# Quadrant tiles for the score pass, v and logits in one pass, and copies moved from ScalarE to VectorE

## The reference

```python
xn = layernorm(x)
q, k, v = split(xn @ w_in.T + b_in)
attn = softmax(q * scale @ k.T + causal)          # per head
a = where(isnan(o), 0, o), o = (attn @ v) @ w_out.T + b_out
scores = softmax(xn @ gate_w.T); combine = the 2 largest, renormalised, * 2.5
g = silu(xn @ w_gate[e]) * (xn @ w_up[e]);  y = sum_e combine[e] * (g @ w_down[e])
out = x + a + y + shared_swiglu(xn)
```

## Time and profile before

| | |
|---|---|
| median of 3 runs | 625.84 us |
| profiled execution | 626.86 us, span 625.1 us |
| TensorE (PE) busy | 553.6 us, 89% |
| VectorE (DVE) | 466.0 us, 75% |
| GpSimd (POOL) | 352.3 us, 56% |
| ScalarE (ACT) | 346.0 us, 55% |
| weight loads (PEld) | 311.6 us, 50% |
| granted TensorE clock, mean | 0.97 of full |

### The profile page before, as it was taken

One profiled execution on the slowest core, in us unless ns is written; L12 is line 12 of the kernel. 1 busy time (PEld: TensorE's weight loads), 2 busy tenths in 40 slices (PEclk: granted clock), 3 DMA queues, 4 the chain that ended last, 5 costly groups with the idle time before them and its releaser, 6 DMA issues.

```text
span 625.1 us, 12489 instructions
## 1 busy us (share of the span) xinstructions
PE 553.6 (89%) x4144; PEld 311.6 (50%) x4144; DVE 466.0 (75%) x781; ACT 346.0 (55%) x472; POOL 352.3 (56%) x357
## 2 busy tenths in 40 slices
PE   1336999999999999999999999999999999999884
PEld 1223664466525664466535664466534664366421
DVE  3974887589785997589775997589776997489602
ACT  1511349733794349733794349733794349733591
POOL 3332764468454764468454774568454774468442
PEclk9757999999999999999999999999999999999897
DMA  5928103540037003450037102450047002450000
GB/s 142 315 60 192 37 1 105 151 138 18 29 126 196 40 17 105 140 146 17 19 134 195 42 17 104 133 154 17 9 144 202 35 17 104 137 152 18 4 2 17
DMA packets 42854, 56.71 MB, mean 91 GB/s; under 512 B 4400, under 2 KB 28304, under 8 KB 42704
## 3 DMA queue, kind: packets, MB, share of 16 engines
q1 hardware_dynamic: 42832, 56.43, 31.0%
HBM read 41.21 MB, written 14.81 MB: 90 GB/s over the span
## 4 chain that ended last, share of the span: by engine, by line
PE 66%; DVE 12%; issue 7%; ACT 5%; SPq 4%; DMA 4%; POOL 1%; POOLq 0%; DVEq 0%; ACTq 0%
PE banks L579 10%; PE banks L450 7%; PE banks L452 6%; PE banks L451 6%; PE banks L552 6%; PE banks L479 6%; PE banks L461 5%; ACT probs L769 5%; PE banks L470 4%; DVE neg_max L1077 4%; PE banks L463 3%; PE banks L462 3%; DMA cb<-c_dram 2%; DVE max_parts L1097 2%; DVE probs L1059 1%
## 5 line engine op out<-in xcount | busy, mean ns | idle before, releaser
L1077 DVE TENSOR_REDUCE neg_max<-banks 128x2 f32<-128x1024 f32 (+3 forms) x224 | 194.6, 914 | 33.7 <-PE banks L470 32.9
L832 POOL TENSOR_TENSOR probs<-probs,cb 128x512 f32<-128x512 f32 x88 | 115.7, 1315 | 77.0 <-ACT probs L721 72.9
L769 ACT ACTIVATE probs<-banks 128x1024 f32<-128x1024 f32 x160 | 154.2, 1032 | 8.6 <-PE banks L552 7.0
L865 POOL TENSOR_SCALAR_AFFINE_SELECT probs<-probs 128x512 f32<-128x512 f32 x128 | 93.3, 749 | 100.0 <-ACT probs L769 99.7
L838 POOL TENSOR_TENSOR hid_lo<-probs,hid_hi 128x512 fp32r<-128x512 f32 (+1 forms) x88 | 112.9, 1284 | 64.9 <-ACT hid_hi L728 64.9
L721 ACT ACTIVATE probs<-banks 128x512 f32<-128x512 f32 (+1 forms) x112 | 66.9, 598 | 143.5 <-PE banks L452 142.2
L1059 DVE TENSOR_TENSOR probs<-probs,banks 128x512 f32<-128x512 f32 (+1 forms) x112 | 75.5, 680 | 34.3 <-PE banks L452 15.1
L450 PE MATMUL banks<-x_hi,w_hi 128*128 128x512 f32 (+1 forms) x224 | 94.1, 420 | 4.5 <-DVE w_lo L1212 2.7
L728 ACT ACTIVATE hid_hi<-probs 128x512 fp32r<-128x512 f32 (+1 forms) x112 | 70.3, 628 | 47.7 <-DVE probs L1059 46.6
L579 PE MATMUL banks<-probs,v_op 128*32 128x512 f32 (+3 forms) x1024 | 95.2, 444 | 0.3
L452 PE MATMUL banks<-x_hi,w_lo 128*128 128x512 f32 (+1 forms) x224 | 89.5, 399 | 0.0
(11 more groups left out here) (114 smaller groups left out, 602.0 us busy)
## 6 DMA issues: line engine op xcount, KB each, us to landing
cb<-c_dram SPq DMA_DIRECT2D x32, 256.0 KB, 4.5
q_op<-q_dram SPq DMA_DIRECT2D x32, 192.0 KB
k_op<-k_dram SPq DMA_DIRECT2D x32, 192.0 KB
cb<-c_dram SPq DMA_DIRECT2D x16, 224.0 KB, 4.6
q_dram<-q_parts SPq DMA_DIRECT2D x8, 384.0 KB, 2.5
k_dram<-k_parts SPq DMA_DIRECT2D x8, 384.0 KB, 2.5
cb<-c_dram SPq DMA_DIRECT2D x16, 192.0 KB, 4.3
cb<-c_dram SPq DMA_DIRECT2D x16, 160.0 KB, 4.6
```

The costliest lines, as they stand in the source:

```text
L769: nc.scalar.activation(probs[:, g % 2, 2 * u:2 * u + 2, :], ring[:, at:at + 2, :], ACT.Exp).then_inc(exp_done, 1)
L832: nc.gpsimd.tensor_tensor(sg[k % 3][:, :], sg[k % 3][:, :], cb[:, TILE_ORDER[k], :], ALU.mult).then_inc(weighted, 1)
L865: return nc.gpsimd.affine_select(out=view, in_=view, compare_op=ALU.is_ge, fill=0.0, base=0, pattern=[[0, 4], [1, P]], channel_multiplier=-1)
L1077: return nc.vector.tensor_reduce(out, in_, AX.X, ALU.max, negate=True)
```

## The change

Five things change together.

1. The tiles of the score pairs are 64 x 64: each head and each mask product is cut in two by the query half c, so that the four combinations of a and c lie on the four quadrants of the array. The mask is one 64 x 64 identity times one triangle of 64 rows; for c = 1 it covers 64 columns in place of 128. A semaphore increment stands in front of each pair.
2. v and the logits come from one set of 4 matmuls of 136 columns, in round 14, into the two banks 4 and 5; q then uses bank 5 (bank 7 in the first block). The routing weights are transposed by one transpose of 128 x 32, and copied as 32 x 128.
3. The pairs come sooner: pairs 0 and 1 stand at the end of `attend`, each ahead of a `gate_up`, and the others in rounds 1 to 10. The first block has two in each of rounds 2 to 11. `ONE_SLOT` is 7. `transpose_on` and `project_out` stand ahead of the late pair of rounds 2 and 3. `find_numbers` and `finish_output` go to round 14.
4. y and q are copied out of their banks by VectorE, behind v and k.
5. SyncE sends the maxima ahead of the store and then waits for the store to land, which `add_tokens` of the next block waits for (`base_free`). Unit 0's exponential, no longer unit 0's matmul, waits for the last hidden tile.

```diff
-PAIRS_AT = [int(k in (1, 11)) + 2 * int(2 <= k <= 10) for k in range(NT + 2)]
-ONE_SLOT = 5
+PAIRS_FIRST = [2 * int(2 <= k <= 11) for k in range(NT + 2)]
+PAIRS_AT = [int(k in (0, 10)) + 2 * int(1 <= k <= 9) for k in range(NT + 2)]
+ONE_SLOT = 7
...
+        vl = banks[:, 4:6, 0:2 * (E + NE)].rearrange("p a (b c) -> p a b c", b=2)
+        q_bank = banks[:, 5, :]
...
-                before(sp, stored, 16 * b)
...
+                maxima_in(i + 1)
                 store(i)
-                maxima_in(i + 1)
+                sp.wait_ge(stored, 16 * i + 16)
+                apart(sp, base_free)
...
+            def project_q(j, bank):
+                if bank is q_bank:
+                    pe.wait_ge(v_done, j + 1)
+                    pe.wait_ge(router_step, ROUTER_STEPS * j + 2)
+                pe.matmul(bank, wqk_sb[:, 0, :], xnT[:, :], start=True, stop=True).then_inc(q_ready, 1)
...
+            def project_v_and_logits(j):
                 pe.wait_ge(xnT_done, j + 1)
                 before(pe, mrows_done, j)
                 for q in range(QT):
-                    mm = pe.matmul(bank_m[:, q * NE:(q + 1) * NE], xnT[:, q * P:(q + 1) * P], gate_sb[:, :],
+                    mm = pe.matmul(vl[:, q // 2, q % 2, :], xnT[:, q * P:(q + 1) * P], wvg_sb[:, :],
                                    start=True, stop=True)
...
-                for q in range(QT):
-                    mm = pe.transpose(bank_m[0:NE, q * P:(q + 1) * P], comb[:, q, :], ident_sb[:, :])
+                pe.transpose(bank_m[0:QT * NE, 0:P], comb[:, :, :].rearrange("p q e -> p (q e)"), ident_sb[:, :]
...
+            def mask_scores(bank, a, c, at, stride, nblk):
                 own = slice(HALF * a, HALF * (a + 1))
+                cols = slice(at % stride + HALF * c, at % stride + P)
+                blocks = bank[HALF * c:HALF * (c + 1), a, :].rearrange("p (k n) -> p k n", n=stride)
+                return pe.matmul(blocks[:, at // stride:at // stride + nblk, cols], ident_half[own, :],
+                                 mask_half[own, 0:P - HALF * c].unsqueeze(1).to_broadcast([HALF, nblk, P - HALF * c]),
+                                 start=False, stop=True, tile_position=(HALF * a, HALF * c), skip_group_check=True)
+            def head_scores(bank, a, c, h, qt, at, first):
                 own = slice(HALF * a, HALF * a + SROWS)
                 n = (qt + 1) * P
+                rows = slice(HALF * c, HALF * (c + 1))
+                pe.matmul(bank[rows, a, at:at + n], q_op[own, h // 2, qt * P + HALF * c:qt * P + HALF * (c + 1)],
+                          k_op[own, h // 2, 0:n], start=first, stop=False,
+                          tile_position=(HALF * a, HALF * c), skip_group_check=True)
...
+                apart(pe, pe_passed)
...
+                    for c in range(2):
+                        for a in range(2):
+                            head_scores(bank, a, c, 4 * g + j + a, qt, at, m == 0)
+                for c in range(2):
                     for a in range(2):
-                for last in range(2):
-                    for a in range(2):
-                        mm = mask_scores(bank, a, *masks, last)
+                        mm = mask_scores(bank, a, c, *masks)
...
-                n = 0
+                pairs_at = PAIRS_FIRST if i is None else PAIRS_AT
+                n = 0 if i is None else EARLY
...
-                    late = int(k < 4 and PAIRS_AT[k] > 1)
-                    for _ in range(PAIRS_AT[k] - late):
+                    ahead = int(k < EARLY and i is not None)
+                    late = int(2 <= k < 4)
+                    for _ in range(pairs_at[k] - ahead - late):
...
                             project_k(b + 1)
-                            logits(b + 1)
+                            project_v_and_logits(b + 1)
...
                     if k >= 2:
                         down(b, k - 2, i)
+                    if k == 2 and i is not None:
+                        transpose_on(i)
+                    if k == 3 and i is not None:
+                        project_out(i)
...
                         if front and g == GROUPS and u in (2, 3):
+                            pair(i + 1, i, u - 2)
                             gate_up(i + 1, u - 2)
...
# ScalarE, attend
+                        if n == 0:
+                            act.wait_ge(hid_done, NT * i + NT)
...
-                        if (g, u) == (0, 1):
-                            take_y(i)
...
-                            if (g, u) == (0, 3):
-                                take_q(i + 1)
...
# VectorE
+            def take_y(i):
+                dve.wait_ge(down_done, NT * i + NT)
+                nc.vector.tensor_copy(yT[:, :], bank_y[:, :]).then_inc(y_taken, 1)
+            def take_q(j):
+                dve.wait_ge(q_ready, j + 1)
+                nc.vector.tensor_scalar(qk_f[:, 0, :], q_bank, QSCALE, bq_scaled[:, 0:1], ALU.mult, ALU.add
+                                        ).then_inc(q_done, 1)
...
-                dve.wait_ge(m_loaded, 32 * b + 32)
+                dve.wait_ge(base_free, b + 1)
...
+                    if k == NT and i is not None:
+                        find_numbers(i)
+                        finish_output(i)
...
-                    for _ in range(PAIRS_AT[k]):
+                    for m in range(pairs_at[k]):
+                        if k == 1 and m == 1 and i is not None:
+                            take_o(i, 1)
                         pair(b, n)
...
                 if front:
+                    take_v(i + 1)
                     split_k(i + 1)
-                    take_v(i + 1)
+                take_y(i)
+                if front:
+                    take_q(i + 1)
                     split_q(i + 1)
```

More of the change, by code:

```diff
@@ L161, in block_kernel @@
         after = 2 * FT + NT * E
-        mask_f = early[:, after:after + 2 * P].rearrange("p (a n) -> p a n", a=2)
-        ident_f = early[:, after + 2 * P:after + 4 * P].rearrange("p (a n) -> p a n", a=2)
+        mask_f = early[:, after:after + P]
+        ident_f = early[:, after + P:after + P + HALF]
         att = probs[:, 0, 0, :].rearrange("p (q e) -> p q e", q=QT)
@@ L257, in block_kernel @@
         summed = sem("summed")
+        base_free = sem("base_free")
         stored = sem("stored")
@@ L406, in project_k @@
                 pe.matmul(nat[:, 1, :], wqk_sb[:, 1, :], xnT[:, :], start=True, stop=True).then_inc(k_ready, 1)
-            def project_q(j):
-                pe.wait_ge(xnT_done, j + 1)
-                pe.matmul(nat[:, 0, :], wqk_sb[:, 0, :], xnT[:, :], start=True, stop=True).then_inc(q_ready, 1)
-            def project_v(j):
-                pe.wait_ge(router_step, ROUTER_STEPS * j + 2)
-                for q in range(QT):
-                    mm = pe.matmul(bank_m[:, q * P:(q + 1) * P], xnT[:, q * P:(q + 1) * P], wv_sb[:, :],
-                                   start=True, stop=True)
-                mm.then_inc(v_ready, 1)
-            def logits(j):
+            def project_q(j, bank):
[4 more added lines that the diff above has]
+            def project_v_and_logits(j):
                 pe.wait_ge(xnT_done, j + 1)
@@ L429, in transpose_comb @@
                 pe.wait_ge(v_done, j + 1)
-                for q in range(QT):
-                    mm = pe.transpose(bank_m[0:NE, q * P:(q + 1) * P], comb[:, q, :], ident_sb[:, :])
-                mm.then_inc(combT_ready, 1)
+                pe.transpose(bank_m[0:QT * NE, 0:P], comb[:, :, :].rearrange("p q e -> p (q e)"), ident_sb[:, :]
+                             ).then_inc(combT_ready, 1)
             def gate_up(b, k):
@@ L637, in experts_and_maxima @@
                         transpose_maxima(b)
-                    if k == 2 and i is not None:
-                        transpose_on(i)
-                    if k == 3 and i is not None:
-                        project_out(i)
             def attend(i, front):
@@ L648, in attend @@
                         if front and (g, u) == (0, 2):
-                            project_q(i + 1)
-                        if front and (g, u) == (0, 3):
-                            project_v(i + 1)
+                            project_q(i + 1, q_bank)
                         if (g, u) == (0, 3):
@@ L665, in _ @@
             transpose_x(0)
-            logits(0)
-            project_q(0)
+            project_v_and_logits(0)
+            project_q(0, bank_y)
             project_k(0)
-            project_v(0)
             transpose_comb(0)
@@ L784, in _ @@
             act.wait_ge(const_made, 1)
-            take_q(0)
+            take_q(0, bank_y)
             take_k(0)
@@ L1157, in experts_and_maxima @@
                         normalise(b + 1)
-                    if k == 1 and i is not None:
-                        take_o(i, 1)
                     if k == 2 and i is not None:
                         normalise_o(i, 1)
-                    for _ in range(PAIRS_AT[k]):
+                    for m in range(pairs_at[k]):
+                        if k == 1 and m == 1 and i is not None:
```

(8 more changed lines are left out.)

70 lines of the change are left out of this document (30 added, 40 removed).

## The result

The changed kernel takes **637.44 us** (median of 4 runs, 633.21 to 640.25), the kernel before 626.54 beside it (625.79 to 628.87): ratio 1.0163, interval 1.0131 to 1.0195. It is slower by 1.6%. The forecast was 617.0 with a range of 604 to 629, so it missed in sign and the time lies outside the range. The profiled execution took 640.25 (span 638.5), the longest of the four, 13.4 over the profiled one of before. Where some of those 13.4 belong to this one execution, I say so.

A forecast was written before the change was run, and what follows sets the result against it. ScalarE was taken to pace stretch A, TensorE to stream through B and wait for VectorE in C. Block 0 -2.4, six periods -4.2, the seventh -1.6 and the tail -0.6 gave -8.8: 617.0 us, range 604 to 629.

The forecast's parts named there:

- A: Stretch from a block's unit 0 (first transposed scores) to gate_up(0): 22.51 us before, forecast 21.85, 0.65 shorter.
- The wait for the store: SyncE waits for the output's store before writing the next k; a store up to 4.5 us is covered, put at nothing.
- ScalarE's 1.27 us: In A, ScalarE loses the copies of y (0.59) and q (0.68); sixteen exponentials end at 20.8 instead of 21.8.
- Stretch B: From gate_up(0) to gate_up(10), with pairs 1 to 18: 33.75 us before, forecast 33.0.
- Pair 4 and pair 7: Remaining waits in B: pair 4 about 0.4 for pair 3, pair 7 about 0.35 for add_attention.
- The four quadrants: Score pairs: one mask matmul per quadrant, all four at once, saves 1.7 us a block; net -1.1 with added costs.
- The 0.3 set aside for pair 10's operands: In B, pair 10 needs the second half of the operands one round sooner: +0.3.
- The rival of late operands: Chance 0.20: pair 0 waits 0.6 and pair 10 1.0 more for loads; +1.6 a period, 628 us.
- Stretch C: From gate_up(10) to the next unit 0: 14.27 before, forecast 14.97, as the split delays hidden(10) and gate_up(12) waits 1.75.
- The rival in which the split is over in 0.9: Chance 0.25: in C the casts fall between GpSimd's instructions, the split takes 0.9 instead of 2.5; 606.5 us.
- The ends: Block 0 -2.4, the seventh period -1.6, after the last unit 0 -0.6 us.
- the seventh period: Last period, without a next block's front; unit 0's 1.34 wait for the maxima's DMA shrinks as they are ready sooner: -1.6.

The follow-up runs named there:

- before: The kernel before the change, measured beside the changed one: 626.54 us.
- f1: The kernel before, with only find_numbers and finish_output moved to round 14 and the maxima's loads ahead of the store on SyncE: 633.12 us, ratio 1.0099.
- after: The changed kernel, with all five parts of the change: 637.44 us, ratio 1.0163.
- e1: The changed kernel with find_numbers back in round 6 and finish_output back in round 8: 636.55 us, ratio 1.0178.
- e2: The changed kernel with split_maxima moved to round 11, behind hidden(10): 624.20 us, ratio 0.9969.
- e4: The changed kernel with y and q copied by ScalarE again, behind the exponentials of units 1 and 3: 633.67 us, ratio 1.0130.
- h1: g1 with take_v(0) behind split_k(0) ahead of the first block: 617.03 us.
- g2: g1 with y and q copied by ScalarE, behind the exponentials of units 1 and 3: 618.67 us.
- e3: The changed kernel with the edits of both e1 and e2: 619.25 us, ratio 0.9903.
- e5: e3 with y and q copied by ScalarE again: 617.93 us, ratio 0.9869.
- q1: The kernel before with only the 64x64 score tiles and the semaphore increment they need: 622.43 us, ratio 0.9931.
- g1: e2 with find_numbers and finish_output one round earlier, in round 13 ahead of hidden(12): 616.94 us, ratio 0.9854.

## Why the prediction was wrong

**The step that failed**, in its words: "find_numbers and finish_output, moved to round 14, fill 1.4 us in which VectorE now waits for GpSimd; they cost nothing, and at most 0.2 if that wait shrinks." Two things were wrong in it. The wait (1.51 in the row of before, not 1.4) ended 1.22 after find_numbers started (313.34 less 312.12), and the steps need 2.8 from start to hidden(13): 1.77, 0.36 of idle time for find_numbers' result, 0.75 less the overlap. And they ran beside the very multiply for which VectorE waits, where a VectorE pass over two operands took 1.77 instead of 0.68. I had priced this collision for the casts of the split and not for the steps that I called free. The Trainium skill ("GPSIMD Engine Reference", Key points) has a rule for it: GpSimd shares its SBUF interfaces with VectorE, and the two contend where a VectorE instruction reads two SBUF inputs or runs in a two-port mode. The traces agree: find_numbers reads att twice and took 1.77, while the reductions of the maxima and the products of hidden, with their operand in a bank, keep their 1.23 and 0.68 beside GpSimd (the reduction at 373.30 ran beside GpSimd's multiply of 372.82). Read against the step, this rule would have warned me.

Alone the step costs 0.63 a period (f1), in the new order 1.03 (after against e1). Whether it also costs at the end is less sure. With the step in round 14 (after, e2, e4, f1) it is 36.3 to 38.4 from the last unit 0 to the end, without it (the nine others) 34.2 to 37.0, and a half clock near that unit 0 stands in all four of the first but also in before, h1 (6.8 us) and g2. So the 4.2 between e2 and e3 belong in part to the execution.

This step is not the whole miss. Seven times 1.03 is 7.2 us; taken off at no price elsewhere it would leave about 630, still slower than before. The rest of A and the ends, below, hold the larger part of the 22.3, and e1 shows that the old places have a price too.

**The rest of A.** Without that step A is 22.76 (e1, e3), 0.91 above the forecast, in three parts. y came at 4.9 after unit 0 and not at 4.5 (in e3), since split_k's last step took 1.00 instead of 0.69, so that transpose_y waits 0.72 and exponential 4 starts at 5.97 instead of 5.5. An exponential takes 0.964 where I took 0.955, and ScalarE stands once more for 0.24. The exponentials end 21.6 after unit 0, hardly sooner than the 21.8 of before, and pair 0 then adds its 0.4. The wait for the store, which I put at nothing, did cost nothing: k's write is issued at 320.28, as split_k ends (319.25 and 1.00). My assumption that ScalarE's 1.27 us come straight off A was wrong: e4 and e5 show that the copies on VectorE lose a little.

**Stretch B** was 0.45 better than forecast. Pair 4 and pair 7 wait 0.42 and 0.46 (forecast 0.4 and 0.35). q1 puts the tiles at 0.9 in B. The four quadrants run at once as taken. The estimate by the Trainium skill ("TensorEngine Tiling (Array Packing)", Instruction Overhead), 13 us for the 512 extra matmuls, does not show: q1 has all of them and is 0.7% faster. The 0.3 set aside for pair 10's operands wasn't needed in the steady blocks. The rival of late operands is not dead, though: in the second period of the profiled execution pair 10 waited for them, and B had 33.79. In e3's fourth period pair 0, too, waited 0.19 for k_op. Pair 10 in the changed kernel:

```profile
215.00 0.41 PE L480 MATMUL banks<-k_op,q_op 48*64 48x512 bf16 x4 [1.04 <-DMA k_op<-k_dram]
```

**Stretch C** was right in mechanism, place and nearly in size: +0.89 for +0.70, and e2 takes all of it away and 0.9 more. I had forecast this loss and still called the whole a gain. The rival in which the split is over in 0.9 was wrong; it takes 2.6 here, and 3.1 in e2.

**The ends.** Forecast -2.4, -1.6 and -0.6; measured +3.5, +0.3 and +2.7 in this execution. Up to the first unit 0 the nine other traces with the new block 0 have 95.7 to 98.6, those with the old one 95.9, 96.3 (q1) and 96.4: about two of the 3.5 us are this execution's own. In the five traces where unit 0 comes after 97.9, a third stretch of half clock lies behind pair 5's wait of 1.43 (here from 68.4 to 71.8). The other five have the same wait of 1.43 and no such stretch, so the wait alone does not decide it. I forecast "about 1" for that wait and not what the clock can do behind it.

k_op came later because its loads were issued 2.0 later (44.57 instead of 42.53), behind the copy of comb (40.02 instead of 38.01); why they then landed 3.3 later is not shown. Of the 2.0, 1.7 are there already when split_k starts (25.43 instead of 23.76): 0.5 at the statistics that wait for x (15.54, 15.01), the rest behind the 0.66 that VectorE now waits for v and the logits and the 0.6 of take_v, which both stand ahead of split_q. The last two steps of split_k ran beside GpSimd (8.2 us for what takes 1.1), but before it was two steps of the router, 2.88 and 3.84 us, and both pairs are ahead of the copy of comb, so this moved k's write, and the copy of comb by 0.4 at most. h1 moves take_v(0) and leaves GpSimd at the same step.

For the seventh period I took the maxima's load to come sooner; in C it came later, with down(11).

**Sum.** Against the forecast, six periods miss by 1.94 in A, -0.45 in B and 0.19 in C (10.1), the irregular early blocks by 1.1, the ends by 5.9, 1.9 and 3.3: 22.3, which is the 13.4 and the 8.8 together, but for rounding. Two sums of the forecast were slightly off in themselves: 33.75 less 0.8 is 32.95 and not 33.0, and the terms listed for block 0 add up to -2.6 and not -2.4.

## What to carry over

A step put "into a wait" of an in-order engine is free only if it ends before that wait does: take its duration beside the engine that one waits for, add the idle time between its own dependent parts, and look who queues behind it. The same two steps cost 1.03 us a period in one round and 0.27 one round earlier. And where a forecast names a loss with its mechanism, test the version without it first: one moved call turned this change from 1.6% slower into 0.3% faster (e2), and a second one made it 1.5% (g1).

## What the runs showed of the hardware

VectorE and GpSimd hold each other up: not_nan 0.68 or 1.77 (GpSimd's multiply 1.70 or 1.30 beside it), casts of 64 elements 0.20 to 1.28, and at the start 4.17 us for a cast that takes 0.43, as long as GpSimd's 3.91 beside it. The long ones end with the GpSimd instruction, or less than one pass behind it (find_numbers at 313.89, the multiply at 313.34). Four matmuls on 64x64 quadrants take the time of one row pair, 0.24. In e1 a wait of 1.56 us in the middle of the kernel was twice followed by 3.4 us at the half clock, which cost 0.9 each; four blocks with the same wait kept the full clock, and in f1 the clock fell once (525.4 to 528.8) where TensorE had waited 0.57 at most since the block's unit 0. So the same order of work can meet the half clock in one block and not in the next, and a few us between two executions can be that alone.
